# Q's units in pairs: two projections, two products with M, eight transposes

## What is computed

```
q = relu(xn @ Wq);  k = relu(xn @ Wk);  v = xn @ Wv        # 32 heads of 64
out_h = (q_h @ (k_h.T @ v_h)) / max(q_h . sum(k_h), 1e-6)  # no softmax
x2 = x + concat(out_h) @ Wo + bo
y  = x2 + MoE(layernorm(x2))      # 8 experts, top 2, gates by softmax of the two scores
```

## Time and profile before

| | us |
|---|---|
| median of 3 runs | 992.87 (992.55 to 995.8) |
| the profiled execution's own time | 993.69 |
| its span, first to last instruction | 992.0 |
| PE busy | 979.3 (99%) |
| DVE busy | 714.3 (72%) |
| ACT busy | 553.7 (56%) |
| POOL busy | 248.5 (25%) |

### The profile page before, as it was taken

The page is one execution under the profiler, slowest core; times in us unless marked ns, Lnnn a source line. Parts: engine busy times, 40 slices in busy tenths (PEclk is TensorE's granted clock), DMA queues, the critical chain, the costliest instruction groups (busy, mean ns, idle before and its releaser), DMA issues.

```text
span 992.0 us, 17230 instructions
## 1 busy us (share of the span) xinstructions
PE 979.3 (99%) x4863; PEld 823.5 (83%) x4863; DVE 714.3 (72%) x1594; ACT 553.7 (56%) x1376; POOL 248.5 (25%) x407
## 2 busy tenths in 40 slices
PE   9999999999999999999999999999999999999997
PEld 7888888888888888888788888888888888888896
DVE  7888665665656676757878787888887786677674
ACT  5445544444445445865556556655555796565553
POOL 1000000000000002221644343444443573433334
PEclk9999999999999999999999999999999999999999
DMA  7012654555555531333221111111114765787773
GB/s 267 4 40 86 212 170 170 170 184 187 188 188 190 188 122 64 107 123 96 86 72 57 53 53 53 53 53 60 56 43 138 230 195 95 119 115 110 119 114 49
DMA packets 121048, 116.15 MB, mean 117 GB/s; under 512 B 47049, under 2 KB 95354, under 8 KB 120866
## 3 DMA queue, kind: packets, MB, share of 16 engines
q1 hardware_dynamic: 111746, 98.51, 32.7%
q0 software_dynamic: 9248, 16.95, 9.1%
HBM read 42.91 MB, written 64.14 MB: 108 GB/s over the span
## 4 chain that ended last, share of the span: by engine, by line
PE 89%; DVE 4%; ACT 3%; DMA 2%; issue 1%; POOL 0%; POOLq 0%; ACTq 0%; DVEq 0%; SPq 0%
PE pK L1739 13%; PE pK L1741 13%; PE pK L1740 13%; PE pA L1739 8%; PE pA L1741 8%; PE pA L1740 8%; PE pX L1739 5%; PE pX L1741 5%; PE pX L1740 5%; PE pA L1873 3%; DMA out<-y,slot_token 2%; PE pT L1819 2%; ACT w_hi L1152 1%; PE pX L2108 1%; PE pT L1754 1%
## 5 line engine op out<-in xcount | busy, mean ns | idle before, releaser
L1006 ACT ACTIVATE qs<-q,nrec 128x64 f32<-128x64 f32 x512 | 129.6, 335 | 88.3 <-DVE nrec L1437 88.2
L622 POOL TENSOR_TENSOR wv_lo<-wv_in,wv_hi 128x512 fp32r<-128x512 f32 x4 | 5.2, 1298 | 403.2 <-ACT wo_hi L927 403.2
L1739 PE MATMUL pA<-k_hi,xn_hi 128*128 128x512 f32 x256 | 101.0, 394 | 0.5 <-DVE k_lo L1312 0.5
L1739 PE MATMUL pK<-wq_hi,xnT_hi 128*128 128x512 f32 x256 | 100.4, 392 | 0.0
L1739 PE MATMUL pK<-wk_hi,xnT_hi 128*128 128x512 f32 (+1 forms) x256 | 100.0, 391 | 0.1
L1741 PE MATMUL pK<-wq_hi,xnT_lo 128*128 128x512 f32 x256 | 99.9, 390 | 0.0
L1741 PE MATMUL pA<-k_hi,xn_lo 128*128 128x512 f32 x256 | 99.8, 390 | 0.0
L1740 PE MATMUL pK<-wk_lo,xnT_hi 128*128 128x512 f32 (+1 forms) x256 | 99.8, 390 | 0.0
L1740 PE MATMUL pK<-wq_lo,xnT_hi 128*128 128x512 f32 x256 | 99.7, 389 | 0.0
L1740 PE MATMUL pA<-k_lo,xn_hi 128*128 128x512 f32 x256 | 99.7, 389 | 0.0
L1741 PE MATMUL pK<-wk_hi,xnT_lo 128*128 128x512 f32 (+1 forms) x256 | 99.6, 389 | 0.0
(11 more groups left out here) (302 smaller groups left out, 2457.3 us busy)
## 6 DMA issues: line engine op xcount, KB each, us to landing
xr_dram<-zero SPq DMA_DIRECT2D x10, 3584.0 KB, 12.8
w_in<-in_ffn_w SPq DMA_DIRECT2D x22, 256.0 KB, 4.0
w_in<-in_ffn_w SPq DMA_DIRECT2D x8, 704.0 KB, 6.5
xn<-in_attn_hidden_states SPq DMA_DIRECT2D x16, 256.0 KB, 5.6
wv_in<-in_attn_Wv SPq DMA_DIRECT2D x16, 256.0 KB, 2.8
wo_in<-in_attn_Wo SPq DMA_DIRECT2D x16, 256.0 KB, 3.0
wk_in<-in_attn_Wq SPq DMA_DIRECT2D x4, 1024.0 KB, 5.7
xnT_dram<-xnT SPq DMA_DIRECT2D x4, 1024.0 KB, 11.7
```

Source lines behind the costliest of these rows:

```text
L1006: i = nc.scalar.activation(qs[:, s], q[:, s], ACT.Copy, scale=nrec[:, b * HC + h:b * HC + h + 1])
L1739: nc.tensor.matmul(dst, lhs[0], rhs[0], start=start, stop=False)
```

## The change

From tile 4 on each engine works two units at a time. PE's order becomes: project(m), project(m+1), [in the second pair of a tile: rank and the wait for `x2_ready`], product(m-2), product(m-1), transposes(m), transposes(m+1). ACT and DVE are put in an order to match, with a tile's other work spread over its two pairs. Unit 15's transposes (and their copies) come before the loops, as the pairs want them; unit 63's come in its pair, ahead of `w_transpose(0)`. Nothing is computed that wasn't, and nothing is left out.

```diff
@@ act
             act_unit(15, 3)
+            act_qsT(15, 1)
 
             def act_tile(t, b):
-                for c in range(NC):
-                    m = 4 * t + c
-                    act_q(m, c % 2)
-                    if c == 0 and not (isinstance(t, int) and t == NT - 1):
+                for p in range(2):
+                    m = 4 * t + 2 * p
+                    act_q(m, 0)
+                    if p == 0 and not (isinstance(t, int) and t == NT - 1):
                         act_qx(t + 1, 1 - b)
-                    act_qsT(m - 1, (c - 1) % 2)
-                    if c == 2:
+                    if p == 1:
                         sqrt_var(NT + t - 1)
-                    act_qs(m, c % 2)
-                    if c == 1:
+                    act_q(m + 1, 1)
+                    act_qs(m, 0)
+                    act_qs(m + 1, 1)
+                    act_qsT(m, 0)
+                    act_qsT(m + 1, 1)
+                    if p == 0:
                         put_planes(t - 2)
...
-            act_qsT(4 * NT - 1, 1)
             put_planes(NT - 2)
@@ dve
-            dots(2, 0, 4)
+            dots(2, 0, 2)
+            dve_qsT(15, 1)
+            dots(2, 2, 4)
 
             def dve_tile(t, b):
-                for c in range(NC):
-                    m = 4 * t + c
-                    if c == 2:
+                for p in range(2):
+                    m = 4 * t + 2 * p
+                    dve_q(m, 2 * p, 0)
+                    if p == 0 and not (isinstance(t, int) and t == NT - 1):
+                        dve_qx(t + 1, 1 - b)
+                    if p == 1:
+                        put_slot8(t - 2, b)
+                    dve_q(m + 1, 2 * p + 1, 1)
+                    if p == 0:
+                        dots(t - 2, 4, E)
+                        put_scores(t - 2)
                         x2_stats(t - 1)
-                    dve_q(m, c, c % 2)
-                    dve_qsT(m - 1, (c - 1) % 2)
-                    if c == 0:
-                        if not (isinstance(t, int) and t == NT - 1):
-                            dve_qx(t + 1, 1 - b)
-                        dots(t - 2, 4, E)
-                    if c == 1:
-                        put_scores(t - 2)
-                    if c == 2:
+                    else:
                         layernorm2(t - 1)
-                    if c == 3:
-                        put_slot8(t - 2, b)
                         dots(t - 1, 0, 4)
+                    dve_qsT(m, 0)
+                    dve_qsT(m + 1, 1)
...
-            dve_qsT(4 * NT - 1, 1)
@@ pe
             def pe_tile(t, b):
-                for c in range(NC):
-                    m = 4 * t + c
-                    project_q(m, t, c, b)
-                    transpose_qs(m - 1, (c - 1) % 2)
-                    if c == 2:
+                for p in range(2):
+                    m = 4 * t + 2 * p
+                    project_q(m, t, 2 * p, b)
+                    project_q(m + 1, t, 2 * p + 1, b)
+                    if p == 1:
+                        rank(t - 2, b)
                         pe.wait_ge(x2_ready, t)
-                    if c == 3:
-                        rank(t - 2, b)
-                    times_m(m - 2, (c - 2) % 4, c % 2, pX[:, :])
+                    times_m(m - 2, (2 * p - 2) % 4, 0, pX[:, :])
+                    times_m(m - 1, (2 * p - 1) % 4, 1, pX[:, :])
+                    transpose_qs(m, 0)
+                    transpose_qs(m + 1, 1)
 
...
                 times_m(10 + c, (c - 2) % 4, c % 2, pX[:, :])
+            transpose_qs(15, 1)
             with pe.Fori(2, NT // 2) as h:
...
             w_transpose(0)
             w_transpose(1)
-            transpose_qs(4 * NT - 1, 1)
             times_m(4 * NT - 2, 2, 0, pX[:, :])
```

## The result

| | before | changed |
|---|---|---|
| median (lowest to highest) of 20 runs each, us | 992.72 (991.83 to 995.8) | 995.61 (993.52 to 997.05) |
| ratio, 95% interval | | 1.0026 [1.0019, 1.0033] |
| profiled execution / its span | 993.69 / 992.0 | 996.94 / 995.2 |
| start of the last product matmul of unit 63 | 781.50 | 785.48 |

The kernel became slower by 2.9 us between the medians, 0.26% (2.6 us) by the ratio: inside the 0.3% that the prediction called no change, and 0.8 above its 994.8. But the interval leaves out 1, and the profile shows that the 2.9 is not made as the sum made it. The experiments are compared with the kernel before as measured beside them, and its runs of 1396 and 3491 us and number 7's of 3492 us, all in the slow state, are left out.

What follows compares the result with a forecast made beforehand. PE's own work plus its waits was taken to bound the stage. Loop part -1.0, rank +0.5, entry +2.7 and exit -0.3 make +1.9 on 992.87, so 994.8 us; 8-in-10 range 993.2 to 998.0.

Steps and rivals of the forecast that it cites:

- Entry, +2.7: Before the loops: transposes(15) start at 490.84 again, without project(16) ahead to fill PE's wait; one projection lost, +2.7 us once.
- Loop part, -1.0: PE's 24 pairs: one return from transposes saved, second four transposes dearer; net 0.04 a pair, -1.0 us.
- Rank, +0.5: Rank between a projection and a product costs 0.17 instead of 0.13, +0.04 a tile over 12 tiles, +0.5 us.
- Exit, -0.3: Unit 63's transposes, weight transposes and wait for qsT_lo before the last products: 1.6 instead of 1.9, -0.3 us.
- No wait in the loops: PE never waits in the loops; qs(m+1) has 1.0 to spare in the first pair, 0.7 in the second.
- Rival 2: Loops: dve_q(m+3) 1.1 late beside put_xb makes PE wait 0.4 in each tile, +4.8, 999.6 us; chance 0.12.
- Granted clock at 1.00 over the gap: Expected sign: PE's clock stays full over the idle 3.5 or so before transposes(15), adding nothing to the sum.
- rival 1: Entry: the idle 3.67 us lowers PE's clock to half, costing 0 to 2.7, taken as 1.7, 996.5; chance 0.17.
- The sum: Whole kernel: entry, loop part, rank and exit together +1.9 us, giving a median of 994.8.
- The likeliest case named: Whole kernel: the forecast itself, 994.8 us with its own range 993.8 to 995.9; chance 0.56.
- Rival 3: Entry costs less, as qs(15) comes sooner or the gap is filled: -0.8 to -1, 992.9 to 994; chance 0.11.
- rival 4: Loops: the second four transposes cost 0.10, not 0.43, gaining 7.9 more over 24 pairs, 986.9 us; chance 0.04.

Runs made afterwards that it cites:

- number 7: Changed kernel with pairs begun one pair sooner, at unit 14, and PE's last two tiles written out after the loop: 990.26 against 993.17 before, 0.9972.
- number 2: Changed kernel with 12 more matmuls, result unused, in the gap before transposes(15): 994.63, ratio 1.0009 to the kernel before.
- number 8: Changed kernel with an added DVE sum in each tile's second pair, over 1536 columns: 998.18, 1.0055; over 2048 columns: 1003.21, run once.
- number 3: Changed kernel with 6 more matmuls, result unused, at the start of the gap before transposes(15): 995.64, ratio 1.0025 to the kernel before.
- number 4: Unit 15's ACT and DVE chain moved forward: in the changed kernel 994.35; there with transposes(15) also back behind project(16) 992.88; in the kernel before 992.76.
- number 1: Changed kernel with transposes(15) back behind project(16), PE's tiles 4 and 5 written out for it: 993.92 against 993.40 before, 1.0005.
- number 5: Changed kernel with PE's tiles 4 and 5 written out and nothing moved: 997.02, ratio 1.0033 to the kernel before.

## Why the prediction came out right, point by point

**Entry, +2.7: right.** Transposes(15) started at 490.99 (predicted: again 490.84), with an idle 3.44 before them, and the marks give the projection's 2.73. PE never got it back.

**Loop part, -1.0: right in kind, a little small.** The kernels that kept the clock have loops and exit at -1.2 to -1.6; the changed order with its entry as it is (number 2) at -1.6, of which the exit is 0.4. That leaves -1.2 for the loops with rank in them, and a tile's length gives the same: 11.81 + 11.92 = 23.73 against 23.84 before, 12 x 0.11 = -1.3. Less rank's +0.1 it is -1.3 to -1.4 for 24 pairs, 0.06 each; predicted was 0.04.

**Rank, +0.5: mis-sized.** It was priced at 0.17 against 0.13, with a full return to the product added. By blocks it is 0.15 in the new place and 0.14 in the old, so the term is +0.1. The products behind the two small matmuls took 0.09 longer, where the return from four transposes takes 0.12.

**Exit, -0.3: right.** 1.13 from the weight transposes on, for 1.27 predicted; with the 0.36 ahead of them 1.49 against 1.9, so -0.4.

**No wait in the loops: right.** The changed kernel's timeline of ACT has `act_qs(m)` and `act_qs(m+1)` back to back in both pairs:

```profile
524.12 4.05 ACT L1006 ACTIVATE qs<-q,nrec 128x64 f32<-128x64 f32 x16
...
535.89 4.05 ACT L1006 ACTIVATE qs<-q,nrec 128x64 f32<-128x64 f32 x16
```

They end at 528.17 and 539.94; the second four transposes begin at about 529.3 and 541.2. That is 1.1 and 1.3 to spare by these rows, where the prediction had 1.0 and 0.7. The second was too low. The prediction made DVE's product `dve_q(m+2)` 1.1 late beside `put_xb`; POOL's timeline of the changed kernel and DVE's have

```profile
532.11 1.29 POOL L642 TENSOR_TENSOR xb<-x_in,bo_b 128x512 f32<-128x512 f32 x1 [0.29 <-POOL vals L693]
```

```profile
531.50 1.26 DVE L1295 TENSOR_TENSOR qsT_lo<-pA,qsT_hi 128x512 fp32r<-128x512 f32 x2
533.31 0.69 DVE L1433 TENSOR_TENSOR qs<-q,ksum 128x512 f32<-128x512 f32 x1 [0.56 <-ACT q L1000]
```

`put_xb` fell where it was laid out: 532.11 is 2.45 behind the start of the second pair (529.66), laid out were 2.5. But it ran beside the two `qsT_lo`, which kept their 0.63 each, and only 0.09 of it was left when the product began, which took its 0.69 here and 0.95 in the next tile, and so on in turn. Rival 2 was thus further off than 0.7: it takes number 8's insertions to bring its wait about, and there 0.5 to 0.65 a tile cost 7.6 in the one run, where the rival had 0.4 a tile for 4.8.

**Granted clock at 1.00 over the gap: wrong; rival 1 came true.** This is the step that failed. The prediction gave it 0.17 and left it out of the sum, on the ground that the one fall it had seen came 3.3 us after the last matmul. Here it came 2.5 us after, and idle pieces of 2.07 and 2.42 sufficed (numbers 3 and 4). Its transposes at the lower level, 0.22 each, were read from the span's start, where those rows give no clock; at a granted 0.50 the trace of the changed kernel has them 0.21 apart, so the reading holds. Its price was taken rightly from the half clock: of 6.83 at half, 5.89 lay on work, worth 2.9 at the most, and 2.7 is measured; of 3.41, all on work, 1.7 at the most, and 1.6 is measured. Over the 20 runs of the changed kernel the mean is 995.5, 1.7 above the two without a fall. Predicted was 1.7 as well, but as a choice between 0 and 2.7, so that it agrees to the tenth is chance.

**The sum.** +2.7 entry, -1.6 loops and exit, +1.7 to 1.8 clock make +2.8 to 2.9, against +1.9 predicted. The likeliest case named was not the one that occurred in most runs. That its number is close is luck: loops, rank and exit together were 0.8 too dear (-0.8 for -1.6), which covers half of the clock that was left out. Rival 3, a cheaper entry, fell with the idle 3.44; rival 4 with groups of eight transposes in 1.03.

## What to carry to other kernels

A loop reordered for a small gain per round is paid for at its seams: look at what the first round now has to wait for, and carry the new order back into the written-out part ahead of it, which here turned +2.9 into -1.9 and, with the last tiles written out, -2.9. Where the engine that is the bound gets a new gap of some 2 to 3.5 us, as the 2.07 to 3.44 here, price the half clock behind it into the sum and not among the rivals; matmuls on operands that are there anyway tell in one run whether it is the clock. And give an experiment that has to write a loop out a control that only writes it out.

## What the runs showed of the hardware that was not expected

- Idle pieces of TensorE of 2.07, 2.42 and 3.44 us brought its clock from 2.4 to 1.2 GHz, in some profiled executions for 3.41 us, in others for 6.83 (after an idle 3.4 both occurred), and by their mean clock in some runs not at all. Shorter pieces never did in the profiled executions: 0.72 and 0.80 at the entry, and 1.45 to 1.81 further on (numbers 1, 4 and 5). The fall can come when the engine is at work again (491.81 in number 3, work from 491.07).
- A VectorE instruction over 8 columns took 1.45 instead of 0.17 beside a GpSimd product over 512 columns that began 0.12 after it, while VectorE's differences that read PSUM and SBUF kept their 0.63 beside the same product.
- A wait of TensorE for `w_lo`, 300 us behind the edited code, showed where two tiles were written out at the front (the stage 33.3) and not where two were written out at the end (31.3); the other kernels lie between, at 31.3 to 32.3, with the same instructions in the stage. What brings it is not shown.
